# Messages kept in place in PSUM, and the sign counts moved to a bank of the destination scores, in a graph attention kernel

## The reference

```
h   = relu(layernorm(x))
xl  = h[n] @ hetero_w[node_type[n]] + hetero_b[node_type[n]]          # 12500 x 32
ete = lrelu(edge_type_emb[edge_type]);  eae = lrelu(edge_attr @ edge_attr_w)
alpha = lrelu(concat(xl[dst], xl[src], ete, eae) @ att_w)
alpha = softmax of alpha over the edges of one dst
msg = concat(xl[src], eae) @ lin_w * alpha
out = x + segment_sum(msg, dst)
```

## Time and profile before

| | us |
|---|---|
| median of 3 runs | 4131.49 (4130.97 to 4132.56) |
| profiled execution, its own time | 4129.91 |
| its span, first to last instruction | 4128.0 |
| busy: POOL | 3089.6 (75%) |
| busy: PE / DVE / ACT | 2477.6 / 2456.1 / 877.7 |
| mean granted TensorE clock | 0.817 of full speed |

### The profile page before, as it was taken

How to read it: one execution, slowest core, us unless ns; L and a number is a source line. 1 busy time by engine, 2 the same in 40 slices (tenths; PEclk the granted TensorE clock), 3 DMA queues, 4 the chain that set the end, 5 groups by cost and what they waited for, 6 DMA issues and landing times.

```text
span 4128.0 us, 50812 instructions
## 1 busy us (share of the span) xinstructions
PE 2477.6 (60%) x14238; PEld 1775.3 (43%) x14238; DVE 2456.1 (59%) x6517; ACT 877.7 (21%) x2080; POOL 3089.6 (75%) x2993
## 2 busy tenths in 40 slices
PE   4476666566566665665665665666656656656510
PEld 3354444444444444444444444444444444444410
DVE  5776565565565665665655656656655656656535
ACT  2131221221221221221222222222222222122100
POOL 0777777777777777777777777777777777777757
PEclk9798788888788888887888888888888888888855
DMA  6432222222222222222222222222222222222122
GB/s 179 110 82 63 58 70 60 58 72 58 58 73 58 60 70 58 67 63 58 71 59 58 72 58 58 73 58 63 67 58 68 62 58 72 58 58 72 27 59 72
DMA packets 194060, 275.76 MB, mean 67 GB/s; under 512 B 78284, under 2 KB 149310, under 8 KB 193152
## 3 DMA queue, kind: packets, MB, share of 16 engines
q1 hardware_dynamic: 72864, 150.69, 12.1%
q0 software_dynamic: 96768, 59.05, 10.5%
q10 hardware_dynamic: 24288, 64.79, 4.3%
HBM read 202.07 MB, written 72.22 MB: 66 GB/s over the span
## 4 chain that ended last, share of the span: by engine, by line
POOL 67%; issue 22%; PE 5%; DVE 3%; DMA 2%; POOLq 1%; SPq 0%; DVEq 0%; ACT 0%; ACTq 0%
POOL gath L491 64%; PE ps_misc L694 2%; POOL hib L531 1%; DMA gath<-table_dram,meta 1%; PE ps_pick L707 1%; DVE node_buf L1145 1%; PE ps_misc L661 1%; POOL hi_f L531 0%; POOL dst_f L531 0%; POOL node_buf L531 0%; PE ps_msg L739 0%; POOLq L488 0%; DVE dscore L1063 0%; PE ps_attr L716 0%; DMA rlast_i<-row_last_in 0%
## 5 line engine op out<-in xcount | busy, mean ns | idle before, releaser
L491 POOL DMA_INDIRECT gath<-table_dram,meta x2875 | 2979.3, 1036 | 969.7 <-issue 869.1
L694 PE MATMUL ps_misc<-parts,dst_f 128*128 128x462 bf16 x5250 | 1124.2, 371 | 239.8 <-DVE h L1050 232.3
L694 PEld LDWEIGHTS ps_misc<-parts,dst_f 128*128 128x128 bf16 x5250 | 514.4, 100 | 787.1 <-DVE h L1050 258.4
L1113 DVE TENSOR_TENSOR node_buf<-gath,ps_msg 128x495 f32<-128x495 f32 x125 | 83.8, 671 | 1132.7 <-DMA gath<-table_dram,meta 1132.7
L750 PE MATMUL ps_msg<-hi_f 128*128 128x98 bf16 x625 | 70.1, 271 | 1105.6 <-DVE node_buf L1115 1105.6
L1063 DVE TENSOR_REDUCE dscore<-ps_pick 128x4 f32<-128x512 f32 x875 | 537.4, 629 | 195.9 <-PE ps_pick L707 195.9
L707 PE MATMUL ps_pick<-s_dst,onehot 122*128 122x128 f32 x3000 | 592.6, 374 | 18.9 <-DVE dscore L1063 17.8
L591 ACT ACTIVATE wts<-args 128x50 f32<-128x50 f32 x125 | 30.7, 246 | 2585.8 <-DVE args L1132 2585.8
L707 PEld LDWEIGHTS ps_pick<-s_dst,onehot 122*128 122x128 f32 x3000 | 560.4, 281 | 42.9 <-DVE dscore L1063 21.7
L750 PEld LDWEIGHTS ps_msg<-hi_f 128*128 128x128 bf16 x625 | 47.0, 127 | 1157.5 <-issue 1156.7
L707 PE MATMUL ps_pick<-s_dst,dst_f 122*128 122x128 f32 x3000 | 382.2, 276 | 21.3 <-DVE dscore L1063 21.3
(11 more groups left out here) (231 smaller groups left out, 1892.6 us busy)
## 6 DMA issues: line engine op xcount, KB each, us to landing
hib<-digit_dram SPq DMA_DIRECT2D x125, 612.5 KB
rows_dram<-rows ACTq DMA_DIRECT2D x125, 437.5 KB, 5.5
gath<-table_dram,meta POOLq DMA_INDIRECT x2875
attr<-edge_attr_t_in SPq DMA_DIRECT2D x125, 200.0 KB
hib<-digit_dram SPq DMA_DIRECT2D x250, 50.0 KB
rows_dram<-gath ACTq DMA_DIRECT2D x1, 8575.0 KB, 47.0
dst_f<-sel_code_dram SPq DMA_DIRECT2D x125, 64.0 KB, 5.3
hib<-digit_dram SPq DMA_DIRECT2D x250, 25.0 KB
```

Source lines behind the costliest of these rows:

```text
L491: nc.gpsimd.indirect_dma_start(gath[u][:, t, :], None, table_dram, bass.IndirectOffsetOnAxis(ap=meta_sb[u][:, t:t + 1], axis=0)).then_inc( ...
L694: last = nc.tensor.matmul(ps_sel[:, j % 2, 0:VW * GN], sel_onehot[:, g, j * P:(j + 1) * P], parts[:, k, g, :], start=(g == 0 and k == 0), ...
```

## The change

- Lines 1113 and 1115 no longer write `msg` in SBUF: the sum is written over the product in `ps_msg` (two parts of 15 and 10 edges, `msg_parts`).
- Alpha reads its column from `ps_msg`: two instructions (15 and 10 edges) for one.
- The product with the weights reads the messages from `ps_msg`: two instructions for one. It still writes `terms` in SBUF, with the features apart by 26 elements.
- A new semaphore `msg_used`, raised by that product, is what PE waits for before it writes the next messages; it waited for `msg_added` and `signs_summed`.
- `ps_signs` moves to bank 1 of `ps_pick`. PE multiplies the signs before `select(*after, 1)` and waits for the pick of group 5 (`SIGNS_AFTER`), no longer for the messages. `dst_scores` of group 1 waits until the signs of the chunk before are summed.
- DVE's `sum_signs(c)` moves from the head of the next chunk to the chain behind the gathers, ahead of line 1138.

```diff
-        msg = in_node_buf(2 * TG * P, [T, VW])
+        ps_signs = ps_pick[:, 1, 0:NPP]
+        msg_parts = [(ps_msg[:, b, 0:n * VW].rearrange("p (t f) -> p t f", f=VW), slice(3 * G * b, 3 * G * b + n))
+                     for b, n in enumerate((3 * G, 2 * G))]
@@ dst_scores (PE)
+                if g == 1:
+                    pe.wait_ge(signs_summed, count(c))
@@ chunk (PE)
-                pe.wait_ge(msg_added, count(c))
-                pe.wait_ge(signs_summed, count(c + 1))
+                pe.wait_ge(msg_used, count(c))
...
-                if not final:
-                    select(*after, 1)
-
                 pe.wait_ge(signs_ready, c + 1)
-                pe.wait_ge(msg_added, count(c + 1))
+                pe.wait_ge(picked, count(c * PICKS + SIGNS_AFTER + 1))
                 for t in range(BPC):
                     last = nc.tensor.matmul(ps_signs, sign_hi[:, t, :], sign_lo[:, t, :], start=(t == 0),
                                             stop=(t == BPC - 1))
                 last.then_inc(signs_mm, 1)
+                if not final:
+                    select(*after, 1)
@@ chunk (DVE)
                 picks(c, 1)
-                sum_signs(c)
-
...
-                v.tensor_tensor(msg[:, 0:3 * G, :], gath[u][:, 0:3 * G, 0:VW],
-                                ps_msg[:, 0, 0:3 * G * VW].rearrange("p (t f) -> p t f", f=VW), ALU.add)
-                v.tensor_tensor(msg[:, 3 * G:T, :], gath[u][:, 3 * G:T, 0:VW],
-                                ps_msg[:, 1, 0:2 * G * VW].rearrange("p (t f) -> p t f", f=VW),
-                                ALU.add).then_inc(msg_added, 1)
+                for part_of_it, tiles in msg_parts:
+                    last = v.tensor_tensor(part_of_it, gath[u][:, tiles, 0:VW], part_of_it, ALU.add)
+                last.then_inc(msg_added, 1)
...
-                k = step(v.tensor_tensor(alpha[:], msg[:, :, F_IN], dscore[:], ALU.add))
+                for part_of_it, tiles in msg_parts:
+                    last = v.tensor_tensor(alpha[:, tiles], part_of_it[:, :, F_IN], dscore[:, tiles], ALU.add)
+                k = step(last)
...
+                sum_signs(c)
                 dve.wait_ge(sums_ready, count(c))
                 v.tensor_copy(terms[:, :, 0:1], sums[:, :, T:T + 1])
...
-                k = step(v.tensor_tensor(terms[:, 0:F_IN, 1:T + 1].rearrange("p f t -> p t f"), msg[:, :, 0:F_IN],
-                                         wts[:, 0, :].unsqueeze(2).broadcast_to([P, T, F_IN]), ALU.mult))
+                for part_of_it, tiles in msg_parts:
+                    last = v.tensor_tensor(terms[:, 0:F_IN, 1 + tiles.start:1 + tiles.stop].rearrange("p f t -> p t f"),
+                                           part_of_it[:, :, 0:F_IN], wts[:, 0, tiles].unsqueeze(2).broadcast_to(
+                                               [P, tiles.stop - tiles.start, F_IN]), ALU.mult)
+                last.then_inc(msg_used, 1)
                 dve.wait_ge(keep_ready, c + 1)
                 dve.wait_ge(rows_sums, count(c))
-                need(k, at)
+                dve.wait_ge(msg_used, count(c + 1))
```

More of the change, by code:

```diff
@@ L34 @@
 PICKS = -(-T // PICK_T)
+SIGNS_AFTER = PICKS - 2
 PART_AT = (0, 12, 24, T)
@@ L171, in gnn_kernel @@
         wts = sb("wts", [P, 2, T])
-        terms = in_node_buf(2 * TG * P + T * VW, [VW, T + 1])
+        terms = in_node_buf(2 * TG * P, [VW, T + 1])
         keep = sb("keep", [P, VW, T + 1])
@@ L240, in gnn_kernel @@
         ps_sel = ps_misc
-        ps_signs = ps_msg[:, 1, 2 * G * VW:2 * G * VW + NPP]
+        ps_signs = ps_pick[:, 1, 0:NPP]
+        msg_parts = [(ps_msg[:, b, 0:n * VW].rearrange("p (t f) -> p t f", f=VW), slice(3 * G * b, 3 * G * b + n))
+                     for b, n in enumerate((3 * G, 2 * G))]
         ps_hmT = [ps_attr, ps_pick]
@@ L300, in gnn_kernel @@
         msg_added = sem("msg_added")
+        msg_used = sem("msg_used")
         onehot_ready = sem("onehot_ready")
@@ L795, in _ @@
             dve.sem_inc(tab_sb, 2)
-            start_at_one(dve, maskT_sb, eae_ready, signs_summed, picked, msg_added, sums_ready, sel_read)
+            start_at_one(dve, maskT_sb, eae_ready, signs_summed, picked, msg_added, msg_used, sums_ready, sel_read)
             steps = [0]
@@ L854, in _ @@
             v.memset(no_rows[:, :, VW + 1:RW], -1.0).then_inc(node_rows_ready, 1)
-            v.memset(ps_signs, 0.0)
             done(v.memset(mrun[:], 0.0))
@@ L1066, in sum_signs @@
             def sum_signs(c):
-                dve.wait_ge(signs_mm, count(c))
+                dve.wait_ge(signs_mm, count(c + 1))
                 dve.wait_ge(signs_summed, count(c))
@@ L1165, in _ @@
             before = steps[0]
-            STEPS = U * 12 + TS_ITER
+            STEPS = U * 11 + TS_ITER
             with dve.Fori(0, ITERS - 1) as i:
@@ L1173, in _ @@
                 chunk(ITERS - 1, u, 0, u == U - 1)
-            sum_signs(CHUNKS)
-            dve.wait_ge(signs_summed, count(CHUNKS + 1))
+            dve.wait_ge(signs_summed, count(CHUNKS))
             done(v.tensor_copy(sign_parts[:, 0, :], sign_sums[:]))
```

## The result

The changed kernel took 4161.06 us (median of 4 runs, 4157.46 to 4166.70), the kernel before 4132.02 us beside it: a ratio of 1.0071, 95% interval 1.0054 to 1.0089. It is slower, by 29 us where 22 were forecast. The profiled execution has a span of 4155.5 us, 27.5 more than before.

A forecast was written before the change was run, and what follows sets the result against it. POOL's unbroken gathers were taken as the bound. Ordinary chunks +28 us, fifth chunks -18 and line 1078 +13 (tail +0.3) gave +23 on 4129.9, 4153; with 1.6 for the runs' median, 4154, range 4050 to 4190.

The forecast's parts named there:

- The bound, and that stretch is all there is: POOL runs its 23 gathers a chunk without a pause; only gather length, with 264 us of stretch, can change the time.
- The product in PSUM holds no gather, and that gains nothing: Gather number 4 is no longer held under the product, but the freed 0.60 us is spent waiting for the scan.
- Rival 3: Stretches add up by instruction: the product's 0.60 goes, the scan's 0.82 stays; -75 us, 4056, chance 0.10.
- The scan starts 0.28 later: In DVE's chain behind the gathers, the scan starts 4.90 us behind line 1113 instead of 4.62.
- The three terms of 0.06, 0.16 and 0.06: Delays in us ahead of the scan: alpha in two 0.06, sum_signs in the chain 0.16, product in two 0.06.
- Ordinary chunks 0.38 longer with line 1078's term: In 100 of 125 chunks gather number 5 is caught again, 0.28 us longer (+28 us); line 1078 adds 0.10.
- Fifth chunks slip, 8 in 10: In 25 chunks number 5 passes before the scan and number 6 is caught, 8 times in 10: -18 us.
- Line 1078's stretch, 0.64 to 0.74: PE begins select at the lower clock level, so line 1078 meets gathers in another phase: +0.10 us a chunk, +13 us.
- The point: Moment in a gather's course when a running two-SBUF-input DVE instruction holds it: put at the gather's start, +-0.10 us.
- rival 1: The scan comes after the point in ordinary chunks too: faster, 4092 if half slip, 4023 if all; chance 0.20.
- slower: The changed kernel's time rises, by +23 us on 4129.9; chance of slower 0.50.

The follow-up runs named there:

- the added instruction: Changed kernel with one more DVE instruction of 98 elements ahead of sum_signs: 4064.96 us, ratio 0.9804, about 4051 on the scale of 4132.
- the control: Kernel before the change with one more DVE instruction of 98 elements ahead of line 1138: 4169.76 us, ratio 1.0053.
- the later one: Later set of runs with the changed kernel, unaltered, against the kernel before: 4144.47 us, ratio 0.9970.

## Why the prediction was right, and where it was not

- *The bound, and that stretch is all there is*: right. The gathers' 27.4 us are the difference of the spans.
- *The product in PSUM holds no gather, and that gains nothing*: right, and shown by the kernel with the messages in SBUF (3.56 us in both). Rival 3 (losses add up by instruction, 4056) is refuted by it and by the added instruction.
- *The scan starts 0.28 later*: 4.67 to 4.95 on average. The three terms of 0.06, 0.16 and 0.06 hold as a sum, but only on average: it was 0.31 in ordinary chunks and 0.13 in fifth ones.
- *Ordinary chunks 0.38 longer with line 1078's term*: 30.67 to 31.09 on average, +0.42, x 100 = 42 us where 38 were forecast (28 and 10). The scan's 0.31 and the 0.11 more under line 1080 make it up.
- *Fifth chunks slip, 8 in 10*: 15 of 23 did, with 2 others. The forecast had number 5 start 0.18 ahead of the scan, well clear. The scan came at 5.00 there and not at 5.14: line 839 started 2.55 behind line 1113 in fifth chunks, and after the change the same instruction (line 842) 2.44 behind line 1114. So number 5 started 0.03 behind the scan on average, and most slipped only because a gather passes up to 0.04 behind it. The number of slips is near the forecast by luck. The chunk fell from 30.96 to 30.40, -0.56 x 25 = -14 us, forecast -0.62 x 25 = -15.
- *Line 1078's stretch, 0.64 to 0.74*: measured 0.63 to 0.74. The 0.64 was made of 0.58 for ordinary and 0.90 for fifth chunks, read from one of each. Over the trace the mean ahead of each of the five chunks of a turn is 0.59 to 0.68, so that split does not exist, and the halfway value was a guess that came out. That `select` begins at the lower level is seen; that this is why the stretch grew is not shown, and the control does not bear it out. The size was right by luck, the cause is open.
- *The point*: put at a gather's start, +-0.10. In the two traces of the changed kernel a gather passed when it began up to 0.043 us behind the scan's start and was caught from 0.045 on. In ordinary chunks number 5 began 0.09 behind it in the median, so they had 0.04 to spare. That was the thin part. I gave rival 1 (ordinary chunks slip too) 0.20 as a doubt about my knowledge; it is a property of the kernel: one instruction more brings it about in nearly all chunks, a landing 0.07 later in some. The added instruction's 4051 on that scale lies inside rival 1's 4023 to 4092. The forecast "slower" holds for the first set of runs and not for the later one: the mechanism was right, the sign hung on 0.04 us.

## What to carry to other kernels

Where an engine that never waits is the bound, ask what lengthens its instructions: the difference between its mean and its median, times the count, was 264 us here, and two operand choices (a scan's input in PSUM, a `tensor_scalar` form) took 6.3% off. Where two engines run to beats that follow each other, a gain or loss is not a sum over instructions: find the event from which the bound engine restarts, and count what gets past it. A time that hangs on a margin of 0.04 us should be forecast as such, and tried with a delay put in: if useless work makes a kernel faster, it sits on an edge.

## What was not expected of the hardware

A scan of 858 elements with one input in PSUM lasts the same 1.94 us as with both in SBUF. DVE's writes with a step of 104 bytes cost 1.83 ns an element in SBUF and 1.05 in PSUM, from the product's parts of 480 and 320 elements (1.07 and 0.78 us, 0.655 and 0.487 us); the whole product took 1.68 us and 1.05. A product with two SBUF inputs over a gather's start held it until 0.68 us behind its own end, a scan until 0.75, and a product that had 0.22 us left cost the gather nothing (0.94 us). The kernel before, unaltered, had medians of 4132, 4146, 4144, 4152 and 4156 us in five sets of runs, two of them on one chip (4146 and 4156). The first set's two traces have the last gather landing at 1.50 us and all later traces at 1.55 to 1.57 (medians); whether that is the reason is not shown.
